# Members of the last step summed by TensorE, and flagged heads kept as bits of one word

## The reference

```python
x = x + xattn(layernorm(x), ctx, ctx)         # sparsemax(q k^T / sqrt(32)) v, then Wo
x = x + ffn(layernorm(x))                     # sqrt((x cos(theta+noise))^2 + (x sin(phi+noise))^2)

def sparsemax(x):                             # over the 722 scores of a row
    zs = sort(x, descending)
    cssv = cumsum(zs) - 1.0
    k = number of i with zs[i] > cssv[i] / i
    tau = cssv[k - 1] / k
    return clip(x - tau, 0)
```

## Time and profile before

| | us |
|---|---|
| median of 3 runs | 723.84 (723.6 to 726.55) |
| the profiled execution | 725.45 |
| its span, first to last instruction | 723.7 |
| TensorE busy in the span | 584.8 (81%) |
| VectorE busy | 609.3 (84%) |
| ScalarE busy | 380.7 (53%) |
| GpSimd busy | 187.1 (26%) |
| mean granted TensorE clock, share of full | 0.902 |

### The profile page before, as it was taken

The page is one execution under the profiler, slowest core; times in us unless marked ns, Lnnn a source line. Parts: engine busy times, 40 slices in busy tenths (PEclk is TensorE's granted clock), DMA queues, the critical chain, the costliest instruction groups (busy, mean ns, idle before and its releaser), DMA issues.

```text
span 723.7 us, 14347 instructions
## 1 busy us (share of the span) xinstructions
PE 584.8 (81%) x4560; PEld 332.5 (46%) x4560; DVE 609.3 (84%) x2964; ACT 380.7 (53%) x657; POOL 187.1 (26%) x239
## 2 busy tenths in 40 slices
PE   3785989798814998899899998990889988997575
PEld 1343545454402654565455544550445544655242
DVE  5699799977966999999999999994899999999600
ACT  3664565766611755666566646560456665563321
POOL 2511403241220240415033502351014430301301
PEclk9879978999965999999999999996899999996857
DMA  9752131202220113130303030303102111200000
GB/s 315 237 166 72 27 103 47 59 0 71 68 76 0 28 28 101 33 84 15 110 26 95 6 105 28 106 1 84 42 1 78 39 45 31 59 17 14 11 1 11
DMA packets 33471, 44.23 MB, mean 61 GB/s; under 512 B 8353, under 2 KB 26785, under 8 KB 33382
## 3 DMA queue, kind: packets, MB, share of 16 engines
q1 hardware_dynamic: 32332, 41.16, 20.0%
q10 hardware_dynamic: 1056, 2.10, 0.8%
HBM read 23.77 MB, written 1.64 MB: 35 GB/s over the span
## 4 chain that ended last, share of the span: by engine, by line
PE 64%; issue 16%; ACT 11%; DVE 4%; SPq 3%; DMA 1%; POOL 1%; POOLq 0%; DVEq 0%
PE ring L456 33%; PE ring L522 8%; PE ring L545 5%; PE ring L599 5%; PE mix_bank L570 5%; PE ring L495 4%; PE ring L507 3%; ACT qst L674 2%; ACT S L674 2%; SPq L248 2%; ACT ctx L674 1%; DMA S<-in_L_xattn_Wk 1%; SPq L252 1%; ACT v L674 1%; ACT ks L682 1%
## 5 line engine op out<-in xcount | busy, mean ns | idle before, releaser
L929 DVE MAX8 cand<-S 100x8 f32<-100x45 f32 (+1 forms) x2048 | 223.1, 188 | 0.5 <-issue 0.4
L456 PE MATMUL ring<-wv,ctx 128*121 128x512 f16 x576 | 156.7, 392 | 0.0
L456 PE MATMUL ring<-ctx,wk 128*128 128x361 f16 x768 | 136.1, 339 | 4.5 <-DVE ctx L1108 4.5
L798 ACT ACTIVATE pT<-ring 121x800 f32<-121x800 f32 x96 | 80.5, 839 | 75.2 <-PE ring L599 75.2
L674 ACT ACTIVATE S<-ring 100x722 f32<-100x722 f32 x128 | 95.2, 774 | 27.6 <-PE ring L545 27.2
L456 PEld LDWEIGHTS ring<-ctx,wk 128*128 128x128 f16 x768 | 78.9, 104 | 58.6 <-issue 14.9
L333 POOL TENSOR_TENSOR ctx<-ctx_f,ctx 128x484 f16<-128x484 f32 x42 | 50.6, 1205 | 163.8 <-ACT ctx L674 163.4
L545 PE MATMUL ring<-kst,qst 96*100 96x361 f16 x256 | 68.0, 361 | 29.4 <-ACT S L674 12.9
L456 PEld LDWEIGHTS ring<-wv,ctx 128*121 128x121 f16 x576 | 71.8, 137 | 33.4 <-issue 7.9
L599 PEld LDWEIGHTS ring<-qst,kst 99*121 99x121 f16 x768 | 61.5, 150 | 45.5 <-issue 21.7
L341 POOL TENSOR_TENSOR ks<-k_f,ks 128x361 f16<-128x361 f32 x64 | 57.2, 894 | 90.9 <-ACT k_f L686 88.2
(11 more groups left out here) (126 smaller groups left out, 727.3 us busy)
## 6 DMA issues: line engine op xcount, KB each, us to landing
kst<-ks SPq DMA_DIRECT2D x384, 45.1 KB, 1.9
ctx_f<-in_ctx SPq DMA_DIRECT2D x45, 242.0 KB, 2.9
xq<-in_x SPq DMA_DIRECT2D x8, 200.0 KB
xr<-in_x SPq DMA_DIRECT2D x8, 200.0 KB
out_y<-att SPq DMA_DIRECT2D x8, 200.0 KB
S<-in_L_xattn_Wk ACTq DMA_DIRECT2D x1, 1024.0 KB, 6.8
wq<-in_L_xattn_Wq ACTq DMA_DIRECT2D x1, 1024.0 KB, 11.3
wcos<-in_L_ffn_theta SPq DMA_DIRECT2D x1, 1024.0 KB, 10.4
```

The source lines that it names most:

```text
L456: last = nc.tensor.matmul(psum, lhs(c, i), w(c, j), start=(c == 0 and n == 0), stop=(c == DC - 1 and n == 2))
L798: nc.scalar.activation(pT[0:CK, u % 3, :, :], src, ACT.Relu).then_inc(two_read, 1)
L929: last = nc.vector.max(cand[:, h, 8 * n:8 * n + 8], S[0:L, HH * (i % 2) + h, cuts[n]:cuts[n + 1]])
```

## The change

VectorE no longer counts the members of the last step. One comparison of all 8 ranks against the new tau writes 1024 marks for each row as bf16, 128 for each head. TensorE sums them over the rows: `n_over` times 1 goes to column 16 of each head, and 8 matmuls, one for each rank r, take the 128 marks of that rank (16 pieces of 8 heads, every 8th element) with weights -1, for the last rank +1, and add up in columns 0 to 15. VectorE then reduces 17 columns for each head. The last step no longer moves tau downwards. The flagged heads become a sum of powers of two, one integer; `settle` loads it once and a loop over 8 heads shifts and masks it. `maxes(i, 0)` waits for the comparison of the half before.

```diff
-        mix_ps, flag_ps = mix_bank[:, 0:L], mix_bank[0:1, P:P + HH]
+        flag_ps = mix_bank[0:1, P:P + HH * (PIECES + 1)].rearrange("p (g n) -> p g n", n=PIECES + 1)
...
-                nc.tensor.matmul(flag_ps, ones[:, :], n_over[:, :], start=True, stop=False)
-                nc.tensor.matmul(flag_ps, minus[:, :], n_now[:, :], start=False, stop=True).then_inc(flag_sum, 1)
+                marks = over[:, :, :].rearrange("p g (n r) -> p g n r", r=8)
+                nc.tensor.matmul(flag_ps[:, :, PIECES], ones[:, :], n_over[:, :], start=True, stop=True)
+                for r in range(8):
+                    last = nc.tensor.matmul(flag_ps[:, :, 0:PIECES], (one_b if r == 7 else minus_b)[:, :],
+                                            marks[:, :, :, r], start=(r == 0), stop=(r == 7))
+                last.then_inc(flag_sum, 1)
...
+                if h == 0 and i > 0:
+                    dve.wait_ge(flag_ready, i)
...
-                counted(nc.vector.tensor_tensor(marks[:, :, :, 7:8], pieces[:, :, :, 7:8],
-                                                t4.broadcast_to([L, HH, PIECES, 1]), ALU.is_lt))
-                n = counted(nc.vector.tensor_tensor(marks[:, :, :, 0:7], pieces[:, :, :, 0:7],
-                                                    t4.broadcast_to([L, HH, PIECES, 7]), ALU.is_ge))
-                after(n)
-                n = counted(nc.vector.tensor_tensor(fold[:, :, 2:2 + NCAND // 2], over[:, :, 0:NCAND // 2],
-                                                    over[:, :, NCAND // 2:NCAND], ALU.add))
-                after(n)
-                n = counted(nc.vector.reduce_sum(n_now[:, :], fold[:, :, :], AX))
-                after(n)
-                nc.vector.scalar_tensor_tensor(n_now[:, :], n_now[:, :], -float(PIECES), n_over[:, :],
-                                               ALU.add, ALU.min).then_inc(flag_ready, 1)
+                nc.vector.scalar_tensor_tensor(t, step_t[:, :], 0.0, t, ALU.max, ALU.add).then_inc(tau_ready, 1)
+                nc.vector.tensor_tensor(marks, pieces, t4.broadcast_to([L, HH, PIECES, 8]), ALU.is_ge).then_inc(flag_ready, 1)
...
-                nc.vector.scalar_tensor_tensor(code[:, :], flag_ps, 0.5, order_c[:, :],
+                nc.vector.reduce_sum(lost[:, :], flag_ps, AX).then_inc(check_step, 1)
+                nc.vector.scalar_tensor_tensor(code[:, :], lost[:, :], 0.5, bit_c[:, :],
-                nc.vector.max(ranked[:, :], code[:, :]).then_inc(check_step, 1)
-                nc.vector.tensor_copy(ranked_i[:, :], ranked[:, :]).then_inc(check_step, 1)
+                    nc.vector.reduce_sum(word_i[:, :], code[:, :], AX).then_inc(check_step, 1)
...
-                    with dve.Fori(0, HH // 2) as pair:
-                        leading = dve.value_load(ranked_i[0:1, bass.ds(2 * pair, 1)], min_val=0, max_val=HH)
-                        with dve.If(leading > 0):
-                            with dve.Fori(0, 2) as k:
-                                number = dve.value_load(ranked_i[0:1, bass.ds(2 * pair + k, 1)], min_val=0, max_val=HH)
-                                with dve.If(number > 0):
-                                    refine(i, number)
+                    with dve.Fori(0, HH) as h:
+                        with dve.If(((word >> h) & 1) > 0):
+                            refine(i, h)
```

More of the change, by code:

```diff
@@ L148, in build_kernel @@
         dif, over = sb("dif", [L, HH, NCAND]), sb("over", [L, HH, NCAND], BF16)
-        fold = sb("fold", [L, HH, 2 + NCAND // 2], BF16)
+        fold = sb("fold", [L, HH, 2 + PIECES * max(RANKS) // 2], BF16)
         tau = sb("tau", [L, 2, HH])
[L151 to L154, removed]
+        f_sum, step_t, n_over = (sb(n, [L, HH]) for n in ("f_sum", "step_t", "n_over"))
+        zero = sb("zero", [L, 1])
+        one_b, minus_b = sb("one_b", [L, 1], BF16), sb("minus_b", [L, 1], BF16)
+        bit_c, code, lost = (sb(n, [1, HH]) for n in ("bit_c", "code", "lost"))
+        word_i = sb("word_i", [1, 1], I32)
         again, againT = sb("again", [P, 32]), sb("againT", [P, 32])
@@ L1012, in test_sums, with refine @@
                 dve.wait_ge(fix, 3 + P // 32)
-            def refine(i, number):
-                number = nc.s_assert_within(number, 1, HH, skip_runtime_bounds_check_because="inside If(number > 0)")
-                t = tau[:, i % 2, bass.ds(number - 1, 1)]
-                row = S[0:L, bass.ds(number - 1 + HH * (i % 2), 1), :].rearrange("p a n -> p (a n)")
+            def refine(i, h):
+                t = tau[:, i % 2, bass.ds(h, 1)]
+                row = S[0:L, bass.ds(h + HH * (i % 2), 1), :].rearrange("p a n -> p (a n)")
                 dve.sem_clear(fix)
@@ L1045, in split_again, with read_flags @@
                 dve.wait_ge(fix, 5)
[L1047 removed]
+            def read_flags(i):
                 dve.sem_clear(check_step)
                 dve.wait_ge(flag_sum, i + 1)
[L1051 removed]
+                nc.vector.reduce_sum(lost[:, :], flag_ps, AX).then_inc(check_step, 1)
+                dve.wait_ge(check_step, 1)
+                nc.vector.scalar_tensor_tensor(code[:, :], lost[:, :], 0.5, bit_c[:, :],
                                                ALU.is_gt, ALU.mult).then_inc(check_step, 1)
[L1053 to L1054 removed]
                 dve.wait_ge(check_step, 2)
[L1056 removed]
+                with nc.allow_low_precision(reason="a sum of distinct powers of two under 256"):
+                    nc.vector.reduce_sum(word_i[:, :], code[:, :], AX).then_inc(check_step, 1)
             def settle(i):
                 dve.wait_ge(check_step, 3)
[L1060 to L1061 removed]
+                word = dve.value_load(word_i[0:1, 0:1], min_val=0, max_val=2 ** HH - 1)
+                with dve.If(word < 1):
                     dve.sem_inc(verified, 1)
[L1063 removed]
+                with dve.If(word > 0):
                     dve.wait_ge(tau_split, i + 1)
[L1065 to L1071 removed]
+                    with dve.Fori(0, HH) as h:
+                        with dve.If(((word >> h) & 1) > 0):
+                            refine(i, h)
                     split_again(i)
@@ L1119, in _ @@
             nc.vector.memset(round_down[:, :], -ROUND).then_inc(dve_const, 1)
[L1120 removed]
+            nc.vector.memset(one_b[:, :], 1.0).then_inc(dve_const, 1)
+            nc.vector.memset(minus_b[:, :], -1.0).then_inc(dve_const, 1)
             for h in range(HH):
[L1122 removed]
+                counted(nc.vector.memset(bit_c[:, h:h + 1], 2.0 ** h))
             n = [counted(nc.vector.memset(again[:, :], 0.0)), counted(nc.vector.memset(zero[:, :], 0.0)),
@@ L1141, in _ @@
                     if h == 3 and i > 0:
-                        rank_flags(i - 1)
+                        read_flags(i - 1)
                     if h == 4 and i > 0:
@@ L1155, in _ @@
                     ln1_apply(b + 1)
-            rank_flags(NH - 1)
+            read_flags(NH - 1)
             settle(NH - 1)
```

12 lines of the change are left out of this document (2 added, 10 removed).

## The result

The changed kernel takes 750.14 us (median of 4 runs, 749.84 to 753.98), the kernel before beside it 724.79 (4 runs, 723.6 to 726.55): ratio 1.0357, 95% interval 1.0321 to 1.0393. It is 3.6% slower. The forecast was 726.1 with a range up to 741.0, so the time lies outside it, on the side of the rival that gave 742.2.

The account below looks back on a forecast made before the run. TensorE was taken to set the pace in steady phases, VectorE mattering only in two corrections and at the end. The terms 8.8 - 4.0 - 2.3 - 0.25 = +2.25 us on the median of 723.84 gave 726.1 us, range 719.5 to 741.

Parts of the forecast that it names:

- the rival that gave 742.2: Mark matmuls: strided reading costs a time for each column, 245 ns a matmul, +18.4 us; chance 0.18.
- What bounds the kernel: Steady phases: TensorE sets the pace, VectorE has about 1 us of slack at each meeting and is on the path in three places.
- x: TensorE's flag sums: time of one of eight new 128-column matmuls, taken as 103 ns between 56 and 245.
- rule of 0.125 us for a ns: Whole run: one ns more for each mark matmul is worth about 0.125 us; break-even near 85 ns.
- The halves that pay: 16 halves less corrections of 3 and 10, the last and half 14: 12 x 0.73 = +8.8 us.
- Half 3: Correction of half 3: starts 1.8 us earlier, loop overhead 2.2 less with empty turns at 0.6; together -4.0 us.
- Half 10: Correction of half 10: starts 0.3 us earlier, loops 2.0 less; together -2.3 us.
- The end: Last test: VectorE's 1.8 us gained, new matmuls counted double at 1.55 us; net -0.25 us.
- The VectorE side: VectorE's test: one comparison of 1.22 us replaces 3.72 us; busy time falls about 30 us, waits for sums and standard deviation grow.
- Free: Mark matmuls: strided reading costs nothing extra, 56 ns a matmul; sum -3.65 us, 720.2 us; chance 0.35.

Follow-up runs that it names:

- sums_added: Kernel before plus only the eight strided mark matmuls in front of the old flag sums, result unused: 752.22 us, ratio 1.0351.
- the pairs: Matmul group added unused to the kernel before, 256 columns as two neighbours out of every 16 bytes: 227 ns a matmul; whole run 820.97 us.
- step 4: Matmul group in the same 820.97 us run on the kernel before, 128 columns at a step of 4 bf16 (8 bytes): 116 ns a matmul.
- step 2: Matmul group in the same 820.97 us run on the kernel before, 128 columns at a step of 2 bf16 (4 bytes): 57 ns a matmul.
- rank_marks: Changed kernel with marks written rank by rank, so the eight matmuls read contiguously: 725.23 us beside 724.71 of the kernel before, ratio 1.0013.

## Why the prediction was wrong, step by step

**What bounds the kernel** was right. TensorE sets the pace, VectorE's saving turns into waiting, and a slower TensorE lengthens every phase: sums_added, in which VectorE does as much as before, is as slow as the changed kernel.

**The step that failed is the cost of a mark matmul, x.** "If the ratio carries over, x is 103 ns; if the time for an element does, x is 245 ns. I take 103 ns, since the reading is of the same kind, and it lies between the ends." The time carries over, nearly: 227 ns. The bounds were right and the choice between them was not. The ratio of 1.84 was VectorE's fetch time divided by VectorE's own pace for an element; TensorE has another pace, so a ratio could not carry over, while a time for fetching from the same memory could. (That the memory sets this time is argued; what is shown is that 1.9 on VectorE and 1.77 on TensorE are close.) The prediction even says so among the rivals, "a line fetched for each column at VectorE's 1.9 ns would be felt more by the faster engine", and gave it 0.18. With 227 in its own terms the sum would be 12 x 1.73 = 20.7, half 3 -3.0, half 10 -1.3 and the end -0.1: +16.3 us, 740.2 instead of 726.1. (Its rule of 0.125 us for a ns gives 741.6; the rule fits below 103 ns; above, the prediction's own rivals make it 0.113, with the end counted once.) So x alone explains 14 us of the miss, and the forecast would have come near its own upper end, not to 750.

In the traces the difference is 26.2 us above the forecast one (28.5 for 2.25): 12.4 in the twelve halves, 4.4 in half 3, 1.7 in half 10, 0.7 at the end, 7.9 in stretches of lower clock, less 0.9 in half 14, the start and the tail. Between the medians the miss is about 3.2 us smaller.

The Trainium skill, "SBUF — State Buffer", section "Door 1: The DMA port swizzle", whose lines of 16 bytes were cited, is borne out in kind: at these steps the cost follows the number of lines touched. Its figure of two hits in a line for full bandwidth is not what TensorE shows here at 2.4 GHz. At two columns for each line (the pairs, and step 4) it runs at half its speed, and at four (step 2) at full speed.

**The halves that pay**: twelve, as forecast. Each pays 1.77 us where 0.73 was forecast and 1.7 follows from x: 21.2 instead of 8.8. Half 14 hides nearly all of its 1.77 behind GpSimd (+0.27), as said.

**Half 3** was forecast at -4.0 and came out at +0.42. Its start: VectorE takes the sums 2.05 us after TensorE reached them, before 2.83; that is -0.78, what the prediction's working gives with the right x (-0.8). Its loops: "six empty turns 3.6" were six at 0.84 us, 5.1. The two loads and their conversion went, but the gaps behind the two jumps, over half of a turn, stayed; the prediction had a turn dearer than 0.6 only in its upper bound. Overhead in and around the corrections is 0.37 + 4.22 + 4.64 = 9.23 us, before 9.0, forecast 6.8. Of the 2.4 us missed, 1.5 are the turns, and most of the rest lies between the two corrections: without two empty turns the 4.22 are 2.5, where the test and the entry were put at 1.6. Of the 1.0 us that is left of the +0.42, 0.8 lie inside the first correction, where VectorE's addition to tau lasts 1.18 and 0.86 us in the two rounds (0.92 and 0.16 before). They end at 212.75 and 216.47, within 0.02 us of the ends of two GpSimd instructions (212.73 and 216.45), so VectorE seems to wait for GpSimd there; no run tests it.

**Half 10** was forecast at -2.3: -0.64. The loops took 8.0 us instead of 9.17, so they gave 1.2 and not 2.0, and the start gave no 0.3 but was 0.8 us later behind TensorE's sums than before (508.39 to 506.33, against the earlier trace rows). There is also a bound that the prediction doesn't have: the correction waits for `tau_split`, which GpSimd raises behind its `ks` subtractions. Where the sums are early this is the last wait. VectorE's timeline in half 3 of rank_marks:

```profile
198.93 0.29 DVE L1049 TENSOR_REDUCE lost<-mix_bank 1x8 f32<-1x136 f32 x1 [0.41 <-PE mix_bank L538]
202.68 0.97 DVE L1018 SCALAR_TENSOR_TENSOR dif<-S,tau,zero 100x722 f32<-100x722 f32 x1 [1.37 <-POOLq L393]
```

VectorE had the sums 0.7 us after TensorE reached them, 2.1 us earlier than before; 1.37 of these were lost to GpSimd.

**The end**: forecast -0.25, measured +0.47. VectorE gave 1.3 us there and the sums took 1.74; eight matmuls at 223 ns, at the low clock the same as at the high one. "I count the new matmuls double" was therefore wrong in kind, but near in size, since 206 was close to 227.

**What the prediction didn't have** is the clock. In the changed kernel's profiled execution 7.9 us lie in stretches with the same work and a lower grant, some 3 of them in that execution only. sums_added loses 27.5 us by its median, but only 21 in its two executions with a mean clock of 0.905, so some 6 us of its loss go with the clock. It comes with strided and contiguous matmuls alike, if 1.8 us of them are added to each half, and is small in the five kernels that don't; with three times as much added it is not larger. Why the grant falls in one stretch and not in the same one of the other kernel stays open.

**The VectorE side** was right: the comparison at 1.22 us (median 1224 ns), the busy time down by 40 us where 30 were forecast, waits for sums and standard deviation up. "Free" as a rival is what rank_marks makes real: forecast 720.2, measured no difference from before. Its 12 x 0.44 us and the end (-1.2 for -1.0) were near the rival's; what it lacks is in half 3 and half 10, which gave 0.65 and 0.97 us where the rival had 4.3 and 2.65.

## What to carry to other kernels

Price a strided operand by the 16-byte pieces that it touches, as a time, and compare that with the engine's own time for its elements; the slower of the two is the cost, and a faster engine feels the same stride more. This is measured for bf16 and steps up to 16 bytes. When one engine writes what another reads, choose the layout for the one that sets the pace: rank_marks moved the stride from TensorE to VectorE and got all 25 us back. Work taken from an engine that waits is worth nothing; here the 0.8% lay in the empty turns of a loop that the pacing engine waits for.

## What the runs showed of the hardware that was not expected

- TensorE's cost of a strided moving side in bf16 does not depend on the clock: 227 ns for 128 pieces of 16 bytes at 2.4 and at 1.2 GHz, and 116 and 115 ns for 64; contiguous it is 56 and 107.
- At 1.2 GHz a step of 8 bytes is therefore almost free (115 beside 107 ns), at 2.4 GHz it doubles the time.
- Output in groups of 16 columns, 17 apart, costs at most 3 ns for 128 columns (59 beside 56).
- An empty turn of a loop with one test takes VectorE's sequencer 0.84 to 0.88 us, of which its six instructions are 0.29.
- Behind 5.5 us of one-column matmuls the granted clock was 0.76 and 24 projections took 5.00 us instead of 3.87; behind the 1.8 us of the changed kernel they did not.
- 1.8 us of strided matmuls added to each half cost 27.5 us over the run by the medians (sums_added), where 12 halves, half 3 and the end make 22.5; the rest appears as stretches of the same work at a lower granted clock.
